# Decoder layer: the gated recurrence's x turned in 32x32 squares by VectorE, its norm factors spread by small products

## The chip, the cores and the metric

The kernel runs on one core of a Trainium2 chip. The metric is the device time of one execution in microseconds (us), lower is better. The core has TensorE (PE, with its weight loads PEld), VectorE (DVE), ScalarE (ACT), GpSimd (POOL) and SyncE (SP), which issues most of the DMAs.

## The reference, cut to what matters

A decoder layer on x of 2 x 2048 x 512 in float32: a gated recurrence, cross-attention, and a mixture of experts. The change touches the first part and the hand-over to the second:

```python
def _layernorm(x, axis=-1, eps=1e-05):
    m = jnp.mean(x, axis=axis, keepdims=True)
    v = jnp.var(x, axis=axis, keepdims=True)
    return (x - m) / jnp.sqrt(v + eps)
...
z = jax.nn.sigmoid(jnp.einsum('bsd,ndk->bsnk', x, Wz) + bz)   # x is layernorm(x) here
h_tilde = jnp.einsum('bsd,ndk->bsnk', x, Wh) + bh
a = (1.0 - z).reshape(b_, s_, d_)
bb = (z * h_tilde).reshape(b_, s_, d_)
_, h = jax.lax.associative_scan(_binop, (a, bb), axis=1)      # h_t = a_t h_(t-1) + bb_t
gate = jax.nn.sigmoid(jnp.einsum('bsd,de->bse', h, Wg) + bg)
return gate * h
```

## The kernel before, in words

The 4096 tokens are worked in 8 chunks of 512 (`NCH = 8`, c = 0 to 7), each of 4 tiles of 128 tokens (`TPC`, index j); the 512 features are 4 blocks of 128 (`KC`, index k for inputs and m for outputs). Every float32 product is done as three products of rounded parts (`TERMS`: high by high, high by low, low by high), so that one block m of z, of h or of the gate is 12 matmuls of 512 columns. ScalarE makes the high part (`hi_part`, L1218), VectorE the low part (`lo_part`, L1615).

The recurrence stage runs from the start to about 327 us. Its order is written out by hand, one list for each engine, tied by semaphores. For each chunk:

- TensorE does `z_and_h(c)`: z0, h0, two turned tiles of the gated rows of the chunk before (`gated_back`, L842), z1, h1, two more of them, z2, h2, z3, h3 (L716). Then `gates(c)`: two groups of transposes of the next chunk's normalised rows (`transpose_x`, L754), the gate products of blocks 0 and 1 without their last input block (18 matmuls, L781), their last input block (6 matmuls), which wait for the low part of h3, the other two groups of transposes, and blocks 2 and 3 (24 matmuls, L781). Block 2 goes into the bank of block 0 and so waits until ScalarE has read block 0 (`gate_ready`). `z_and_h(c + 1)` waits for the last low part of x.
- ScalarE, for each m: high part of h(m - 1), then the sigmoid of z(m) (L1284). Then high part of h3, high parts 0 and 1 of the next x, gate sigmoids 0 and 1 (L1301), high parts 2 and 3 of x, gate sigmoids 2 and 3, with pieces of the expert weights (`split_piece_hi`) between.
- VectorE, for each m: low part of h(m - 1), then `recurrence(c, m)`: b (L1680), a = 1 - z (L1683), the scan (L1686), the carry (L1689). Between them lie the residual rows and statistics of the chunk before. Then low part of h3, a weight piece, low parts 0 and 1 of x, `gated` 0 and 1 (L1714), low parts 2 and 3 of x, the rest, the statistics of chunk c + 2 (`ln1_stats`, L1646 to L1652) and its normalised rows (`ln1_apply`, L1658).
- GpSimd makes the inverse deviation (`ln1_pow`, L2564). SyncE moves weight pieces, rows of x and results; it also places the keys (`kblk`) at the start.

Chunk 0 has its own start: TensorE turns its x between the products of keys and values. The statistics of chunk 1 are taken in chunk 0, behind recurrence 1.

## Time and profile before

| | |
|---|---|
| median of 3 runs | 1172.0 us (1169.74 to 1174.47) |
| the profiled execution, its own time | 1170.26 us |
| its span, first to last instruction | 1168.5 us |
| mean granted TensorE clock | 0.991 |
| busy share of the span | PE 95%, DVE 78%, PEld 77%, ACT 62%, POOL 34% |
| one chunk of the recurrence | 36.57 us |

The span is 1.8 us short of the execution's own time. The shares are means over stages with different limits; for this change the recurrence stage alone is to be read.

### The profile page before, as it was taken

What the parts mean: (1) busy time and instruction counts of PE and PEld (TensorE: products, weight loads), DVE (VectorE), ACT (ScalarE), POOL (GpSimd) and SP (SyncE); (2) the same over time, 40 slices, a digit from 0 to 9 for tenths busy, and PEclk for the clock granted to TensorE, in tenths of its full rate; (3) what the DMA queues carried; (4) which work ended last, traced back from release to release, by engine and by line L of the source; (5) the groups of instructions that cost most, each with busy time, mean ns of one, the idle gap of its engine ahead of it and who ended that gap; (6) DMA issues with size and microseconds to landing.
All of it is one profiled execution on the core that took longest, in us unless ns stands there. A gap on an engine that the chain in (4) does not pass through costs nothing.

```text
span 1168.5 us, 24237 instructions
## 1 busy us (share of the span) xinstructions
PE 1108.3 (95%) x6017; PEld 905.0 (77%) x6018; DVE 910.5 (78%) x2172; ACT 722.2 (62%) x2148; POOL 393.4 (34%) x328
## 2 busy tenths in 40 slices
PE   6999999999989999999999888999999999999993
PEld 5888888888877787777777666777888888888882
DVE  6888888887874778878878877877777777777774
ACT  5223332233377777768676644866787787877873
POOL 3000000000034433545536364445534434443432
PEclk9999999999999999999999998999999999999998
DMA  8544545445340133143143377786555454444543
GB/s 261 163 149 159 190 148 173 151 163 207 126 147 1 57 89 111 56 124 100 46 145 90 128 206 219 201 249 152 94 85 81 81 85 80 86 81 81 88 63 40
DMA packets 95316, 144.76 MB, mean 124 GB/s; under 512 B 20864, under 2 KB 37428, under 8 KB 94607
## 3 DMA queue, kind: packets, MB, share of 16 engines
q1 hardware_dynamic: 77338, 106.83, 28.8%
q0 software_dynamic: 17216, 35.73, 17.4%
q10 hardware_dynamic: 693, 1.36, 0.4%
q8 instruction: 33, 0.54, 0.2%
q14 instruction: 36, 0.29, 0.1%
HBM read 82.69 MB, written 64.76 MB: 126 GB/s over the span
## 4 chain that ended last, share of the span: by engine, by line
PE 72%; DVE 9%; issue 7%; DMA 6%; ACT 3%; POOL 2%; DVEq 0%; POOLq 0%; ACTq 0%; SPq 0%
PE banks L1126 27%; PE banks L716 17%; PE banks L928 7%; PE banks L781 6%; DMA out<-rows,scatter_rows 4%; PE banks L893 3%; PE banks L906 3%; PE banks L1154 2%; PE banks L1138 2%; ACT rows L1335 2%; DVE operands L1615 2%; PE banks L917 1%; PE banks L754 1%; DVE rows L1917 1%; ACT operands L1218 1%
## 5 line engine op out<-in xcount | busy, mean ns | idle before, releaser
L1126 PE MATMUL banks<-operands 128*128 x1608 | 390.5, 398 | 9.2 <-ACT operands L1218 5.0
L1126 PEld LDWEIGHTS banks<-operands 128*128 128x128 f32 x1608 | 299.5, 190 | 73.9 <-issue 14.2
L716 PE MATMUL banks<-operands 128*128 128x512 f32 (+2 forms) x1224 | 290.1, 393 | 3.6 <-DVE operands L1615 3.6
L716 PEld LDWEIGHTS banks<-operands 128*128 128x128 f32 (+1 forms) x1224 | 226.1, 192 | 48.3 <-DVE operands L1615 3.7
L1218 ACT ACTIVATE operands<-banks 128x512 fp32r<-128x512 f32 (+1 forms) x232 | 137.6, 602 | 63.4 <-PE banks L807 34.2
L1615 DVE TENSOR_TENSOR operands<-banks,operands 128x512 fp32r<-128x512 f32 (+1 forms) x232 | 156.7, 683 | 15.6 <-ACT operands L1218 12.2
L1335 ACT ACTIVATE rows<-banks,score_shift 128x77 f32<-128x77 f32 x512 | 158.4, 337 | 11.2 <-DVE score_shift L1839 10.9
L2686 POOL DMA_INDIRECT out<-rows,scatter_rows x67 | 106.4, 1588 | 155.3 <-DVE rows L2419 109.7
L1218 ACT ACTIVATE operands<-rows 128x512 fp32r<-128x512 f32 (+2 forms) x77 | 54.0, 710 | 163.6 <-DVE rows L1686 139.4
L1540 ACT ACTIVATE banks<-banks,param_cols 128x128 f32<-128x128 f32 x268 | 99.2, 431 | 82.2 <-PE banks L1154 75.6
L2357 DVE BATCH_NORM_STATS2 moe_stats<-banks 128x6 f32<-128x512 f32 x134 | 93.2, 696 | 37.5 <-PE banks L1126 31.5
L2595 POOL TENSOR_TENSOR rows<-rows,score_rec 128x1232 f32<-128x1232 f32 x32 | 72.9, 2278 | 142.6 <-DVE score_rec L1847 142.6
L1335 ACT ACTIVATION_READ_ACCUMULATOR rows<-banks,score_shift 128x1 f32 x512 | 111.7, 218 | 0.0
L2660 POOL DMA_INDIRECT rows<-xf_rows,gather_rows x67 | 67.3, 1005 | 101.7 <-DVE gather_rows L2384 87.0
L928 PE MATMUL banks<-operands 128*128 128x512 f32 x384 | 94.2, 397 | 0.0
L781 PE MATMUL banks<-operands 128*128 128x512 f32 x384 | 91.9, 395 | 0.1
L781 PEld LDWEIGHTS banks<-operands 128*128 128x128 f32 x384 | 70.9, 188 | 15.8 <-DVE operands L1615 1.2
L928 PEld LDWEIGHTS banks<-operands 128*128 128x128 f32 x384 | 70.3, 188 | 14.9 <-DVE rows L1872 0.7
L906 PE MATMUL banks<-ident,rows 128*77 128x128 f32 x512 | 69.6, 276 | 11.3 <-DVE operands L1615 7.5
L906 PEld LDWEIGHTS banks<-ident,rows 128*77 128x77 f32 x512 | 58.4, 147 | 28.1 <-issue 13.7
L2569 POOL TENSOR_TENSOR ln_rstd<-ln_var_eps,minus_half 128x4 f32 (+1 forms) x8 | 10.1, 1260 | 181.1 <-DVE ln_var_eps L1710 181.1
L2608 POOL DMA_INDIRECT slot_table<-slot_payload,slot_rows x64 | 63.5, 991 | 19.2 <-issue 16.9
(191 smaller groups left out, 1603.1 us busy)
## 6 DMA issues: line engine op xcount, KB each, us to landing
expert_parts<-operands SPq DMA_DIRECT2D x32, 512.0 KB, 3.0
operands<-expert_parts SPq DMA_DIRECT2D x8, 2048.0 KB, 11.4
rows<-in_x SPq DMA_DIRECT2D x8, 1024.0 KB, 5.5
rows<-in_L_ffn_W SPq DMA_DIRECT2D x32, 256.0 KB, 3.6
x_rows<-rows SPq DMA_DIRECT2D x8, 1024.0 KB, 4.3
rows<-x_rows SPq DMA_DIRECT2D x8, 1024.0 KB, 6.2
xf_rows<-rows SPq DMA_DIRECT2D x32, 256.0 KB
out<-rows SPq DMA_DIRECT2D x32, 256.0 KB
```

What stands on the lines that cost most here:

```text
L716: last = nc.tensor.matmul(dst, stationary(a, k), moving(b, k), start=(t == 0 and k == 0), stop=(t == len(terms) - 1 and k == n_k - 1))
L781: last = nc.tensor.matmul(g_bank[m % 2], wg[:, a, k, m * P:(m + 1) * P], hTr[:, a2, k, :], start=(k == 0 and t == 0), stop=(k == KC - 1 an ...
L906: last = nc.tensor.transpose(tb(c, f"p{m}{hl}")[0:SK, j * P:(j + 1) * P], pb[m % 2][:, j, hl * SK:(hl + 1) * SK], ident[:, :])
L928: last = nc.tensor.matmul(mb(at, f"o{j}"), out_part(c, a, m)[:, j * P:(j + 1) * P], wo[:, a2, m, :], start=(m == 0 and t == 0), stop=(m == ...
L1126: last = nc.tensor.matmul(dst, stationary[:, a, k, :], weights[:, w, bass.ds(e, 1), a2, k, :].rearrange("p e f -> p (e f)"), start=False, ...
L1218: return nc.scalar.activation(dst, src, ACT.Copy, scale=scale)
L1335: nc.scalar.activation(pb[m % 2][:, j, keys], s_banks[:, j, keys], ACT.Exp, bias=nmax[:, m % 2, at], scale=-1.0, accum_out=ssum[:, m % 2, ...
L1540: nc.scalar.activation(ch_bank[:, at], ch_bank[:, at], ACT.Relu, scale=pcol[:, bass.ds(e * KC + (ROW_G1 + k), 1)], bias=pcol[:, bass.ds(e ...
L1615: return V.tensor_tensor(dst, src, hi.bitcast(F32), ALU.subtract)
L2357: V.bn_stats(c_st[:, which, :], src).then_inc(stat, 1)
L2595: G.tensor_tensor(p3, p3, srec[:, m % 2, :].unsqueeze(2).to_broadcast([P, TPC * HPG, SK]), ALU.mult).then_inc(p_ready, 1)
L2686: G.indirect_dma_start(out, bass.IndirectOffsetOnAxis(six[u][:, 0:1], 0), y2[u], None, compute_op=ALU.add).then_inc(added[u], 16)
```

## The change

- Rows of x are loaded a second time, in 32x32 squares (`load_squares`, four DMAs for each chunk into `xn`), from chunk 1 on. ScalarE normalises them in place (`normalise_x`): 4 x 4 activations of 128x128 with a scale and a bias, tiles 0 and 1 behind the sigmoid of z2, tiles 2 and 3 behind that of z3 (chunk 0: behind z3 and behind the high part of h3). VectorE turns them (`turn_x`): tiles 0 and 1 behind recurrence 3, tiles 2 and 3 behind the low part of h3 (chunk 0: all four there). `transpose_x` and `ln1_apply` are gone; chunk 0's own x is still turned by TensorE.
- The scale and bias of every row have to reach the partition of its square: GpSimd multiplies rstd with the negated mean, TensorE spreads both with four products of 8 columns (`spread_scales(c + 1)`, behind h1; in chunk 0 behind h2), VectorE copies the result out.
- a = 1 - z is made by ScalarE behind each sigmoid, into a tile of its own (`za_left`).
- The features of x come in another order, so Wz and Wh are loaded by 16 DMAs each in place of 4.
- The buffers of the squares lie where the keys are placed (`kblk`); the keys wait in DRAM (`kT_d`) and are placed in chunk 7, and GpSimd clears `kblk` there in two memsets.
- Some semaphores are merged (`passed`, `setup_t_done`, `ln1_stat`); their waits keep their places.

```diff
+
+
+        Q = nc.alloc_sbuf_tensor_at("recurrence_rows", [P, 77 * KB_ // 4], F32, offset=r_base + 48 * 1024)
+        xT_rows = Q[:, 0:KC * CH].rearrange("p (k t) -> p k t", k=KC)
+        sc1 = Q[:, 8 * KB_:8 * KB_ + 2 * TPC].rearrange("p (s j) -> p s j", s=2)
+        sc1_cols = Q[:, 8 * KB_:8 * KB_ + 2 * TPC]
+        sc_sq_cols = Q[:, 9 * KB_:9 * KB_ + 2 * CH // SQ]
+        sc_sq = sc_sq_cols.rearrange("p (b s j) -> p b s j", b=P // SQ, s=2)
+
+        spread = Q[:, 10 * KB_:12 * KB_].rearrange("p (b q r) -> p b q r", b=P // SQ, q=KC)
+        za_left = Q[:, 61 * KB_ // 4:77 * KB_ // 4].rearrange("p (i t) -> p i t", i=2)
...
             for raw, name, loaded in ((raw_wz, "L0_attn_Wz", wz_in), (raw_wh, "L0_attn_Wh", wh_in)):
                 for n in range(KC):
-                    sp.dma_start(raw[:, :, n * P:(n + 1) * P],
-                                 io[name][n].rearrange("(k p) f -> p k f", p=P)).then_inc(loaded, 16)
+                    for q in range(KC):
+                        sp.dma_start(raw[q * SQ:(q + 1) * SQ, :, n * P:(n + 1) * P],
+                                     io[name][n][q * P:(q + 1) * P, :].rearrange("(k r) f -> r k f", r=SQ)).then_inc(
+                            loaded, 16)
...
+            def load_squares(c):
+                src = x_sq[c] if isinstance(c, int) else x_sq[bass.ds(c, 1)].rearrange("c r b f -> (c r) b f")
+                for q in range(KC):
+                    sp.dma_start(xn[q * SQ:(q + 1) * SQ].rearrange("p j (b f) -> p (j b) f", f=P),
+                                 src[:, :, q * P:(q + 1) * P]).then_inc(xp_in, 16)
...
+                        sp.dma_start(kblk[rows, a, :, :, hl * SK:(hl + 1) * SK].bitcast(F32),
+                                     kT_d[rows, a]).then_inc(k_placed, 16)
...
             sp.wait_ge(k_lo, KC)
-            for hl in range(HPG):
-                rows = slice(hl * DH, (hl + 1) * DH)
-                for a in (HI, LO):
-                    sp.dma_start(kblk[rows, a, :, :, hl * SK:(hl + 1) * SK].bitcast(F32),
-                                 kT[rows, a].bitcast(F32)).then_inc(k_placed, 16)
+            sp.dma_start(kT_d, kT[:, :, :, :, :].bitcast(F32)).then_inc(k_placed, 16)
...
+            sp.wait_ge(a_t_done, KC)
+            load_squares(1)
...
             def a_chunk(c, first):
+                c_squares = not isinstance(c, int) or c < NCH - 2
...
+                    if n == 3 and c_squares:
+                        need_alone(sp, x_turned, 4 * (c + 1), passed)
+                        load_squares(c + 2)
+                    if n == 3 and isinstance(c, int) and c == NCH - 1:
+                        place_keys()
...
-            def transpose_x(c, ks=range(KC)):
-
+            def transpose_first(ks):
...
+            def spread_scales(c):
+
+                pe.wait_ge(ln1_rstd, rstd_steps(c))
+                need(pe, gate_ready, 4 * (c - 1))
+                for b in range(P // SQ):
+                    last = nc.tensor.matmul(g_bank[0][:, b * 2 * TPC:(b + 1) * 2 * TPC],
+                                            spread[:, b].rearrange("p q r -> p (q r)"), sc1_cols, start=True, stop=True)
+                last.then_inc(sc_done, 1)
+
             def z_and_h(c, back=True):
...
-                pe.wait_ge(a_t_read, t_group(c) + 4)
+                if isinstance(c, int) and c == 0:
+                    pe.wait_ge(a_t_read, KC)
+                else:
+                    pe.wait_ge(xnT_lo, 4 * c)
...
+                    if m == (1 if back else 2) and not (isinstance(c, int) and c == NCH - 1):
+                        spread_scales(c + 1)
...
-                if ahead:
-                    transpose_x(c + 1, (0, 1))
-                else:
+                if not ahead:
...
                     if m == 0:
+                        if ahead:
+                            pe.wait_ge(sc_in, c + 1)
...
                 pe.wait_ge(hT_lo, 4 * c + KC)
                 for m in range(2):
                     gate_terms(c, m, (KC - 1,)).then_inc(g_done, 1)
-                if ahead:
-                    transpose_x(c + 1, (2, 3))
-                else:
+                if not ahead:
                     x1_to_features(0, -1, (2, 3))
                 for m in range(2, KC):
                     pe.wait_ge(gate_ready, 4 * c + m - 1)
...
-            def x_hi(c, ks=range(KC)):
...
+            def x_hi(c, ks):
+                if ks[0] == 0:
+                    act.wait_ge(h_done, 4 * c)
+                    act.wait_ge(x_turned, 4 * c)
+                for k in ks:
+                    hi_part(xnT[:, HI, k, :], xT_rows[:, k, :]).then_inc(xnT_hi, 1)
+
+            def normalise_x(c, js):
+                for j in js:
+                    if j == 0:
+                        act.wait_ge(xp_in, 16 * KC * c)
+                        act.wait_ge(sc_in, c)
+                    for b in range(P // SQ):
+                        square = xn[:, j, b * P:(b + 1) * P]
+                        last = nc.scalar.activation(square, square, ACT.Identity, scale=sc_sq[:, b, 0, j:j + 1],
+                                                    bias=sc_sq[:, b, 1, j:j + 1])
+                    last.then_inc(xn_ready, 1)
...
                     need(act, h_ready, n - 1)
                     nc.scalar.activation(za[:, m % 2, :], z_bank[m % 2], ACT.Sigmoid,
                                          bias=pcol[:, ROW_BZ + m:ROW_BZ + m + 1]).then_inc(z_ready, 1)
+                    act.wait_ge(z_ready, n + 1)
+                    nc.scalar.activation(za_left[:, m % 2, :], za[:, m % 2, :], ACT.Identity, scale=-1.0,
+                                         bias=ones[:, 0:1]).then_inc(a_ready, 1)
+                    if not last:
+                        normalise_x(c + 1, ((), (), (), (0, 1))[m] if first else ((), (), (0, 1), (2, 3))[m])
...
                 h_hi(c, KC - 1)
+                if first:
+                    normalise_x(c + 1, (2, 3))
...
             def ln1_stats(c):
-                need(dve, xn_ready, 4 * c)
-                need_alone(dve, x_in, 16 * (c + 1), dve_passed)
+                need_alone(dve, x_in, 16 * (c + 1), passed)
                 for j in range(TPC):
...
-                need_alone(dve, ln1_stat, 4 * (c + 1), dve_passed)
+                need_alone(dve, ln1_stat, 8 * c + 4, passed)
+                need_alone(dve, xn_ready, 4 * c, passed)
+                if not (isinstance(c, int) and c < 2):
+                    need_alone(dve, sc_in, c - 1, passed)
                 for j in range(TPC):
-                    V.bn_aggr(mv1[:, j, :], st1[:, j, :]).then_inc(ln1_aggr, 1)
...
+                if not (isinstance(c, int) and c == 0):
+                    V.tensor_scalar(sc1[:, 1, :], mv1[:, :, 0], -1.0, None, ALU.mult)
                 V.tensor_scalar_add(ve1[:, :], mv1[:, :, 1], EPS).then_inc(ln1_eps, 1)
 
-            def ln1_apply(c):
-                dve.wait_ge(ln1_rstd, c + 1)
-                need(dve, a_t_done, t_group(c - 1) + 4 if not (isinstance(c, int) and c == 0) else 0)
+            def first_rows():
...
-                    V.tensor_scalar(xn[:, j, :], xr(c, j), mv1[:, j, 0:1], rs1[:, j:j + 1],
-                                    ALU.subtract, ALU.mult).then_inc(xn_ready, 1)
...
+            def turn_x(c, js):
+                for j in js:
+                    dve.wait_ge(xn_ready, 4 * c + j + 1)
+                    V.transpose(xT_rows[:, :, j * P:(j + 1) * P].rearrange("p k (b r) -> p b k r", r=SQ),
+                                xn[:, j].rearrange("p (b k r) -> p b k r", b=KC, k=KC)).then_inc(x_turned, 1)
...
+            def x_lo(c, ks):
                 for k in ks:
                     dve.wait_ge(xnT_hi, 4 * c + k + 1)
-                    lo_part(xnT[:, LO, k, :], t_bank[k % 2], xnT[:, HI, k, :]).then_inc(a_t_read, 1)
+                    lo_part(xnT[:, LO, k, :], xT_rows[:, k, :], xnT[:, HI, k, :]).then_inc(xnT_lo, 1)
...
@@ -1680,10 +1757,9 @@
                 V.scalar_tensor_tensor(zb, h_bank[m % 2], pcol[:, ROW_BH + m:ROW_BH + m + 1],
                                        za[:, m % 2, :], ALU.add, ALU.mult).then_inc(b_ready, 1)
                 dve.wait_ge(b_ready, n + 1)
-                V.tensor_scalar(za[:, m % 2, :], za[:, m % 2, :], -1.0, 1.0, ALU.mult, ALU.add).then_inc(a_ready, 1)
                 dve.wait_ge(a_ready, n + 1)
                 need(dve, carry_ready, n - 3)
-                V.tensor_tensor_scan(hT[:, m, :], za[:, m % 2, :], zb, carry_at(c, m, 0),
+                V.tensor_tensor_scan(hT[:, m, :], za_left[:, m % 2, :], zb, carry_at(c, m, 0),
                                      ALU.mult, ALU.add).then_inc(h_ready, 1)
...
                     if first and m == 1:
-                        dve.wait_ge(k_placed, 16 * 2 * HPG)
+                        dve.wait_ge(k_placed, 16)
+                        V.tensor_copy(spread, ident[:, :].rearrange("p (b r) -> p b r", r=SQ).unsqueeze(2).to_broadcast(
+                            [P, P // SQ, KC, SQ]))
                     if m:
                         h_lo(c, m - 1)
                     recurrence(c, m)
                     if first and m == 1:
                         ln1_stats(1)
+                    if ahead and m == (2 if first else 1):
+                        dve.wait_ge(sc_done, c + 1)
+                        V.tensor_copy(sc_sq_cols, g_bank[0][:, 0:CH // SQ * 2]).then_inc(sc_in, 1)
                     if m == (2 if first else 1):
                         split_piece_lo(c, 0)
-                    if first and m == 2:
-                        ln1_apply(1)
...
+                    if ahead:
+                        turn_x(c + 1, ((), (), (), ())[m] if first else ((), (), (), (0, 1))[m])
                 h_lo(c, KC - 1)
+                if ahead:
+                    turn_x(c + 1, (0, 1, 2, 3) if first else (2, 3))
                 split_piece_lo(c, 1)
...
-                if ahead >= 2:
-                    ln1_apply(c + 2)
...
             def ln1_pow(c):
                 pool.wait_ge(ln1_eps, c + 1)
-                need(pool, xn_ready, 4 * c)
-                G.tensor_tensor(rs1[:, :], ve1[:, :], half[:, 0:TPC], ALU.pow).then_inc(ln1_rstd, 1)
+                if isinstance(c, int) and c == 0:
+                    G.tensor_tensor(rs1[:, :], ve1[:, :], half[:, 0:TPC], ALU.pow).then_inc(ln1_rstd, 1)
+                    return
+                G.tensor_tensor(sc1[:, 0, :], ve1[:, :], half[:, 0:TPC], ALU.pow).then_inc(ln1_rstd, 1)
+                pool.wait_ge(ln1_rstd, rstd_steps(c) - 1)
+                G.tensor_tensor(sc1[:, 1, :], sc1[:, 1, :], sc1[:, 0, :], ALU.mult).then_inc(ln1_rstd, 1)
...
+            pool.wait_ge(xnT_lo, 4 * (NCH - 1))
+            G.memset(r_at(48, int(15.25 * KB_)).bitcast(F32), 0.0)
+            pool.wait_ge(h_ready, KC * NCH)
+            G.memset(r_at(63.25, 4 * KB_).bitcast(F32), 0.0).then_inc(pool_step, 1)
```

## Rows read from the trace of the kernel before

**Rows 1.** The page's first part, one engine: busy us, share, instructions.

```profile
PE 1108.3 (95%) x6017; PEld 905.0 (77%) x6018; DVE 910.5 (78%) x2172; ACT 722.2 (62%) x2148; POOL 393.4 (34%) x328
```

**Rows 2.** Busy time from behind h3 of chunk 1 to chunk 2's; clock, DMA share last.

```profile
88.05:124.62 36.57, 36.57 (x177) 30.37 (x176) 31.52 (x60) 12.26 (x22) 2.50 (x2) 1.00 0.48 165
```

**Rows 3.** Timeline of TensorE, chunk 2: start, us, work, count, idle before.

```profile
113.61 11.17 PE L716 MATMUL banks<-operands 128*128 128x512 f32 x48
124.62 1.03 PE L754 MATMUL banks<-ident,rows 128*128 128x128 f32 x8
125.62 5.78 PE L781 MATMUL banks<-operands 128*128 128x512 f32 x24
131.24 1.04 PE L754 MATMUL banks<-ident,rows 128*128 128x128 f32 x8
132.03 5.73 PE L781 MATMUL banks<-operands 128*128 128x512 f32 x24
```

**Rows 4.** Timeline of VectorE, the same chunk, behind h3.

```profile
125.48 0.75 DVE L1680 SCALAR_TENSOR_TENSOR rows<-banks,param_cols,rows 128x512 f32<-128x512 f32 x1
126.26 0.45 DVE L1683 TENSOR_SCALAR rows<-rows 128x512 f32<-128x512 f32 x1
126.85 1.28 DVE L1686 TENSOR_TENSOR_SCAN rows<-rows,carry 128x512 f32<-128x512 f32 x1
128.28 0.15 DVE L1689 COPY carry<-rows 128x1 f32 x1
128.84 1.29 DVE L1615 TENSOR_TENSOR operands<-rows,operands 128x512 fp32r<-128x512 f32 x2 [0.40 <-ACT operands L1218]
```

**Rows 5.** Timeline of ScalarE, the same chunk.

```profile
124.45 0.67 ACT L1284 ACTIVATE rows<-banks,param_cols 128x512 f32<-128x512 f32 x1
128.71 1.07 ACT L1218 ACTIVATE operands<-banks 128x512 fp32r<-128x512 f32 x2
130.75 1.38 ACT L1301 ACTIVATE rows<-banks,param_cols 128x512 f32<-128x512 f32 x2 [0.97 <-PE banks L781]
```

**Rows 6.** Groups by line behind 327 us: count, busy, mean ns, idle.

```profile
L1917 DVE STREAM_TRANSPOSE rows<-rows 128x512 f32<-128x512 f32 x24 | 15.4, 681 | 0.0
L1540 ACT ACTIVATE banks<-banks,param_cols 128x128 f32<-128x128 f32 x268 | 99.2, 431 | 82.2 <-PE banks L1154 75.6 <-issue 6.6
```

**Rows 7.** Timeline of TensorE: two narrow float32 products of a later stage.

```profile
433.58 0.29 PE L961 MATMUL banks<-gate_sel,before 128*128 128x16 f32 x2
...
433.95 1.09 PE L893 MATMUL banks<-operands 128*128 128x308 f32 x6
```

**Rows 8.** Timeline of TensorE, the start and chunk 0.

```profile
26.27 24.83 PE L716 MATMUL banks<-operands 128*77 128x512 f32 x108
50.94 1.77 PE L754 MATMUL banks<-ident,rows 128*128 128x128 f32 x8
...
58.90 1.40 PE L781 MATMUL banks<-operands 128*128 128x512 f32 x5
```

**Rows 9.** Timeline of VectorE in chunk 0.

```profile
34.88 0.75 DVE L1680 SCALAR_TENSOR_TENSOR rows<-banks,param_cols,rows 128x512 f32<-128x512 f32 x1 [1.57 <-PE banks L716]
...
46.07 0.17 DVE L1652 TENSOR_SCALAR ln_var_eps<-ln_mean_var 128x4 f32<-128x4 f32 x1
```

**Rows 10.** Timeline of GpSimd in chunk 0.

```profile
46.32 1.67 POOL L2564 TENSOR_TENSOR ln_rstd<-ln_var_eps,minus_half 128x4 f32<-128x4 f32 x1 [20.50 <-DVE ln_var_eps L1652]
```

**Rows 11.** Timeline of TensorE in the expert stage: 12 matmuls behind a wait.

```profile
708.00 4.50 PE L1126 MATMUL banks<-operands 128*128 x12 [2.22 <-ACT banks L1516]
...
737.08 3.00 PE L1126 MATMUL banks<-operands 128*128 x12 [0.89 <-ACT operands L1218]
```

**Rows 12.** Timeline of TensorE in chunk 7.

```profile
307.34 2.04 PE L807 MATMUL banks<-ident,rows 128*128 128x128 f32 x8
```

**Rows 13.** Timeline of SyncE's queue at the start.

```profile
12.30 4.97 SPq L464 DMA_DIRECT2D rows<-in_L_attn_Wh  x4
```

**Rows 14.** Timeline of ScalarE at the start.

```profile
18.38 1.92 ACT L1218 ACTIVATE operands<-rows 128x2048 fp32r<-128x2048 f32 x1 [2.15 <-DMA rows<-in_L_attn_Wz]
```

122 lines of the change are left out of this document (67 added, 55 removed).

## The prediction

> **What bounds the kernel now.** The page's first part comes first: TensorE is busy 95% of the span, VectorE 78% [rows 1]. That is a mean over stages, so the stretches come next. From behind h3 of chunk 1 to behind h3 of chunk 2, TensorE is busy 36.57 of 36.57 us, VectorE 31.52, ScalarE 12.26, at full clock [rows 2]. So TensorE sets the time of the recurrence stage, and a microsecond saved or lost in its row is one of the kernel's. VectorE, 86% busy, is near enough that where its work stands in its list decides. The timelines then show who is last at each turn [rows 3, 4, 5]. All times below are of chunk 2; T is the end of h3 in TensorE's row, 124.62.
>
> TensorE before: transposes of x from T to T + 1.00, gate blocks 0 and 1 to T + 6.62, transposes to T + 7.41, blocks 2 and 3 from there [rows 3]. One 512-column matmul advances the row by 11.01 / 48 = 0.23 us. ScalarE sigmoids gate 0 at 130.75, before TensorE wants its bank at 132.03 [rows 3, 5]. VectorE has the low part of h3 at about 129.5, TensorE wants it at about 125.62 + 18 x 0.23 = 129.8 [rows 3, 4]. So the transposes that go are work, but they also stand where TensorE would otherwise wait for the other two.
>
> **The steady chunk (1 to 6), part by part.** *Removed from TensorE:* 16 transposes, 1.00 + 0.79 = 1.8 us [rows 3].
>
> *Added to TensorE:* four float32 products of 8 columns. Two such products of 16 columns advance the row by 433.95 - 433.58 = 0.37 us [rows 7], so four cost 0.75; I take 0.8. Bounds 0.5 and 1.0: the columns are half as many, but the weights are as wide.
>
> *VectorE:* loses four times 0.43 (a = 1 - z, [rows 4]) and the four normalised rows, gains four turns of 15.4 / 24 = 0.64 [rows 6] and two small copies. It comes out a little lighter, and no longer runs behind the recurrences: in chunk 2 it began the last one at 125.48, 0.86 after T [rows 4]. The products of chunk 0 show how early it can begin: 36 matmuls from 26.27 end at 34.5, and b starts at 34.88, 0.35 later [rows 8, 9].
>
> *ScalarE:* gains 16 squares. The nearest row is the 128x128 activation with scale and bias, 99.2 / 268 = 0.37 us in a row of them [rows 6]; bounds 0.3 and 0.5. With four activations of 512 columns (0.6 each) this is 8.3 us in a chunk, on 12.3 busy of 36.57 [rows 2]. Behind z3 (T - 2.75, read from T - 2.4) stand the sigmoid 0.6, a 0.7, eight squares 3.0 and a weight piece 0.6: ScalarE is free at T + 2.5, when the scan of h3 ends. No loss; at 0.5 for a square it is T + 3.5, still hidden by VectorE's turning.
>
> The Trainium skill speaks against this move: its page ScalarE: Activation LUTs, section Rules for kernel authors, sends multiplies and adds to VectorE, and budgets 0.3 us for an activation plus 0.83 ns for an element, 0.41 us for a square. The trace agrees with its budget within a tenth (0.37 to 0.43), and by it the squares would cost 6.5 us of ScalarE in place of 5.9, with no change in the sum.
>
> *The new wait.* Follow VectorE and ScalarE from T, with the durations and gaps of [rows 4, 5, 6]:
> - b from T + 0.35 to 1.1; scan 1.25 to 2.55; carry to 2.85.
> - turns of tiles 0 and 1, 2 x 0.62: to 4.1. The high part of h3 is ready at 3.1, so it waits for the turns, not they for it.
> - low part of h3: to 4.8. TensorE has done its 18 matmuls at T + 4.15: it waits about 0.7, and its blocks 0 and 1 end at T + 6.2.
> - turns of tiles 2 and 3: to T + 6.05. Only now may ScalarE take the high parts 0 and 1 of x (they need all four tiles), 1.1 us: to 7.15; gate sigmoid 0: to 7.85.
> - TensorE's block 2 needs the bank that this sigmoid empties: it starts at T + 7.9 and waits 1.7.
>
> Before it started at T + 7.41. The 1.8 us that went out come back as waits of 2.4, so blocks 2 and 3 begin 0.5 later than before, and the spreading products come on top: a chunk takes 36.57 + 0.5 + 0.8 = 37.9, +1.3. Six chunks: **+7.8**. What stands behind is in time: low parts 2 and 3 of x at about T + 10.5, wanted at T + 13.5.
>
> *DMAs:* SyncE passes `x_turned` together with the weight piece behind it, which VectorE makes only after the turns, and issues four loads of squares. At the 1.24 us of each of the four Wh loads [rows 13] that is at most 5 us of queue, about T + 6.5 to T + 11.5. The squares are first read 30 us later. The expert piece queued behind them is read at about T + 14: hidden. The DMA engines are busy 0.48 [rows 2]; 1 MB more a chunk lifts that by a few tenths.
>
> **Chunk 0.** T here is 50.94 [rows 8]. The spreading products stand behind h2, at 26.27 + 84 x 0.23 = 45.5, but the statistics of chunk 1 are ready only at 46.07 + 0.17 [rows 9]. VectorE saves one 0.43 and gains a small product: 45.9. GpSimd's power takes 1.67 [rows 10]: 47.65. Its new product of 4 columns has no row; it lies between nothing and 1.67, I take 0.8 (same shape, simpler operation). TensorE spreads at 48.5, 3.0 us late, so T becomes 54.9: **+4.0**. Then all four tiles are turned behind h3: ScalarE's squares 0 and 1 wait for the scales and z3, squares 2 and 3 stand behind the high part of h3 and end at about 61.0; the last turn 61.7, high parts 62.8, sigmoid 63.5. Block 2 starts at T + 8.65 where it was 58.90 - 50.94 = 7.96 [rows 8]: **+0.7**, in a wait of 3.1.
>
> *The clock.* Behind a wait of 2.22 us, 12 matmuls take 4.50 us; behind one of 0.89 they take 3.00 [rows 11]. The longer wait cost 1.5 more behind it. Chunk 0 has two waits of 3.0, longer still: **+3.0**. A steady chunk's 0.7 and 1.7, apart by 1.4 of work, lie between the two rows; I take no fall, bounds 0 and 1.5.
>
> **The start.** Wz and Wh now come by 32 DMAs. The bytes and pieces are the same; four issues of Wh took 4.97 us [rows 13], and sixteen of a quarter's size take somewhat more. ScalarE already waited 2.15 for Wz [rows 14], and the low parts that start z0 follow closely. I take **+1.0**; bounds 0 and 3.
>
> **Chunk 7.** In its 2.04 us for 8 transposes of x1 against 1.03 in others [rows 3, 12] TensorE waits for VectorE's rows, and VectorE is lighter by 0.43 a block: **-1.0**, bounds -1.0 and 0. The keys are placed in this chunk, some 5.4 us of queue from about T + 7; TensorE wants them at about T + 17: nothing, but 2 or 3 us of cover.
>
> **The sum.** 7.8 + 4.7 + 3.0 + 1.0 - 1.0 = 15.5 on 1170.26 gives 1185.8. The median of the runs is 1.7 above that execution: 1187. What lies behind the recurrence stage is unchanged and starts later by the same.
>
> **The rivals.**
> 1. *The clock falls in every chunk* (0.18). The waits of 0.7 and 1.7 bring it down. For: the 4.50 behind 2.22. Against: the 3.00 behind 0.89 [rows 11]. Price 6 x 1.5 = 9: 1196. The Trainium skill, TensorE: Matmul & The Clock Gate, section The HAM clock gate, has the array fall to 1.2 GHz when it idles; the 4.50 us against 3.00 agree with the rule.
> 2. *The wait for gate 0 does not arise* (0.17). It would take ScalarE's sigmoid before T + 5.6, 2.3 us earlier than the list above gives. Then a steady chunk is 0.8 - 1.8 = -1.0, six -6; chunk 0 +4.0 - 2.4 + 1.5 of one fallen clock = 3.1; start +1, chunk 7 -1: -3, **1169**, no change.
> 3. *The same, and faster* (0.10): the sign turns when in addition the unknown prices lie at their low ends: GpSimd's product 0.1 in place of 0.8, nothing at the start, no fallen clock. That is -3.0 - 0.7 - 1.0 - 1.5 = -6.2: **1166**. Each steady chunk must then wait less than 0.1 in all. For it speaks that TensorE has 1.0 less to do in 36.57 us and VectorE is lighter; against it the order: two turns stand before the low part of h3 and four before the gate's sigmoid.
>
> **How the numbers follow.** The forecast (waits as worked out, clock falling in chunk 0 alone) has 0.55, with 1179 to 1192 as its own range: the steady chunk at +0.6 to +1.8 (squares 0.3 to 0.5, products 0.5 to 1.0), start 0 to 3. Two in ten lie outside 1170 to 1197. Half a per cent, 5.9 us, is about what a measurement of this kernel tells from no change. Faster 0.10; same (rival 2 and the low edge of the forecast) 0.18; slower 0.72.
>
> **What the changed profile would show.** TensorE idle twice in each `gates`: some 0.7 us before the last input block of blocks 0 and 1, released by the low part of h3, and 1.7 before block 2, released by the gate's sigmoid. The second is the heart: without it the forecast falls to rival 2. In chunk 0 an idle of 3 us before the spreading products, released by GpSimd. A granted clock below 1.00 in the steady stretches would say rival 1. A turn of far less than 0.64 us, or squares over 0.5, would move the waits by four or eight times the difference.

## The result, and the profile after

The changed kernel takes 1193.4 us (median of 4 runs, 1187.6 to 1197.3) against 1172.2 before: the ratio is 1.0183, 95% interval 1.0157 to 1.0210. The forecast was 1187, slower: 6 too low. The measured time lies 1.4 above the 1179 to 1192 that the prediction gave its main line, and inside its wider 1170 to 1197. The profiled execution took 1192.81 us, its span 1191.0, so 22.5 us more than the span before.

The page's first part after the change, to be held against [rows 1]:

```profile
PE 1110.4 (93%) x5961; PEld 904.5 (76%) x5962; DVE 906.1 (76%) x2155; ACT 788.9 (66%) x2292; POOL 397.0 (33%) x336
```

All shares fell by a little while the span grew: TensorE was given waits. The windows of the changed kernel say where. Columns: length; busy time of TensorE, its weight load, VectorE, ScalarE, GpSimd; granted clock; DMA share; GB/s. The second runs from h3 of chunk 1 to h3 of chunk 2 and answers to [rows 2]; the others are 4 us behind a wait in chunk 0 and in chunk 7.

```profile
53.00:57.00 4.00, 4.00 (x13) 3.47 (x14) 1.39 (x3) 0.23 (x1) 0.00 (x0) 0.50 0.19 70
102.01:140.00 37.99, 35.87 (x169) 29.43 (x168) 30.78 (x58) 21.46 (x42) 3.10 (x3) 1.00 0.61 186
331.00:335.00 4.00, 4.00 (x14) 3.35 (x15) 3.42 (x6) 1.50 (x3) 0.95 (x1) 0.57 0.07 28
```

This first steady chunk is 37.99 us long instead of 36.57 (the ones behind it 37.6 to 37.8) and TensorE is busy for 0.7 less in it, at a granted clock of 1.00 (the level of 2.4 GHz). In the other two TensorE is never idle, but at 0.50 (1.2 GHz) and 0.57.

TensorE's timeline of the changed kernel: first the start and chunk 0, then chunk 2 (T = 140.00), then chunk 7. In brackets stands the idle time before a group and what ended it.

```profile
31.25 18.00 PE L743 MATMUL banks<-operands 128*128 128x512 f32 x72 [2.55 <-DVE operands L1677]
52.61 1.88 PE L788 MATMUL banks<-recurrence_rows 128*128 128x8 f32 x8 [3.36 <-POOL recurrence_rows L2648]
54.34 7.49 PE L743 MATMUL banks<-operands 128*128 128x512 f32 x24
...
70.42 7.35 PE L820 MATMUL banks<-operands 128*128 128x512 f32 x24 [3.15 <-ACT rows L1363]
...
127.37 0.95 PE L788 MATMUL banks<-recurrence_rows 128*128 128x8 f32 x8
140.00 4.24 PE L820 MATMUL banks<-operands 128*128 128x512 f32 x18
144.75 1.66 PE L820 MATMUL banks<-operands 128*128 128x512 f32 x6 [0.50 <-DVE operands L1677]
147.78 5.75 PE L820 MATMUL banks<-operands 128*128 128x512 f32 x24 [1.37 <-ACT rows L1363]
...
327.32 0.38 PE L846 MATMUL banks<-ident,rows 128*128 128x128 f32 x2
330.49 1.54 PE L846 MATMUL banks<-ident,rows 128*128 128x128 f32 x6 [2.79 <-DVE rows L1803]
331.68 7.08 PE L820 MATMUL banks<-operands 128*128 128x512 f32 x24
```

Read chunk 2 first, against [rows 3]. The two groups of transposes of x are gone. In place of the first stands nothing, of the second two idle times: 0.50 before the last six matmuls of blocks 0 and 1 (VectorE's low part of h3), and 1.37 before block 2 (ScalarE's gate sigmoid). Block 2 starts at T + 7.78. Chunk 0 shows the same in larger: 3.36 for GpSimd's factors, 3.15 for the sigmoid, and behind each a group of 24 matmuls takes 7.3 to 7.5 us where it takes 5.6 at full clock.

Why the sigmoid is late is seen in the other engines' timelines. VectorE of the changed kernel behind h3 (compare [rows 4]):

```profile
140.26 0.75 DVE L1757 SCALAR_TENSOR_TENSOR rows<-banks,param_cols,rows 128x512 f32<-128x512 f32 x1 [1.57 <-PE banks L743]
141.15 1.28 DVE L1762 TENSOR_TENSOR_SCAN rows<-recurrence_rows,carry,rows 128x512 f32<-128x512 f32 x1
142.81 1.30 DVE L1730 STREAM_TRANSPOSE recurrence_rows<-rows 128x512 f32<-128x512 f32 x2
144.04 0.65 DVE L1677 TENSOR_TENSOR operands<-rows,operands 128x512 fp32r<-128x512 f32 x1
144.61 1.29 DVE L1730 STREAM_TRANSPOSE recurrence_rows<-rows 128x512 f32<-128x512 f32 x2
```

ScalarE of the changed kernel, the same place (compare [rows 5]):

```profile
138.90 3.18 ACT L1286 ACTIVATE rows<-rows,recurrence_rows 128x128 f32<-128x128 f32 x8
141.99 1.14 ACT L1255 ACTIVATE operands<-rows 128x512 fp32r<-128x512 f32 x2
146.00 1.15 ACT L1255 ACTIVATE operands<-recurrence_rows 128x512 fp32r<-128x512 f32 x2 [2.87 <-DVE recurrence_rows L1730]
147.06 1.25 ACT L1363 ACTIVATE rows<-banks,param_cols 128x512 f32<-128x512 f32 x2
```

The last turn ends at 145.90, T + 5.90, where the prediction had T + 6.05; ScalarE has stood still for 2.87 us and takes the high parts of x at 146.00; only then the two sigmoids, from 147.06; and TensorE goes on at 147.78. The sigmoid's bank was full before that: where it stands first in the list (experiment 1) it starts 1.00 behind the restart of TensorE's last six matmuls, which would be 145.75 here, 1.3 earlier. So an operand of the *next* chunk stands in ScalarE's list ahead of the gate that *this* chunk's next matmuls wait for.

**Where 23.7 us went**, read as differences of the starts of the same groups in TensorE's row, after minus before, up to the last gate block of chunk 7 (339.39 against 315.67):

| stretch | measured | forecast |
|---|---|---|
| start: z0 at 31.25 in place of 26.27 + 12 x 0.23 = 29.0; then 72 matmuls in 18.00 in place of 16.5 | +2.2, +1.5 | +1.0 |
| chunk 0: wait 3.4, spreading products 1.7, z3 and h3 at the low clock +1.8, gate products 15.94 in place of 13.5, +2.4 | +9.3 | +7.7 |
| chunks 1 to 6 (six recurrence steps) | +6.8 | +7.8 |
| chunk 7's gate products | +3.7 | -1.0 |

The stages behind it gave back 1.2, and 22.5 are left.

### The profile page after: what moved, and what is told of

Read it like the earlier page. It is cut to its first block, busy times and chain, and to the rows that moved or that the text cites. A ratio compares the mean times of both kernels' runs of the same rounds, so it can differ in the third digit from the quotient of the medians.

```text
span 1191.0 us, 24340 instructions
## 1 busy us (share of the span) xinstructions
PE 1110.4 (93%) x5961; PEld 904.5 (76%) x5962; DVE 906.1 (76%) x2155; ACT 788.9 (66%) x2292; POOL 397.0 (33%) x336
## 4 chain that ended last, share of the span: by engine, by line
PE 65%; DVE 10%; issue 8%; DMA 6%; ACT 4%; SPq 3%; POOL 2%; another core or an unknown queue 0%; DVEq 0%; POOLq 0%; ACTq 0%
PE banks L1163 25%; PE banks L743 18%; PE banks L965 5%; PE banks L820 4%; PE banks L930 3%; PE banks L943 3%; DMA rows<-slot_table 2%; DMA out<-rows,scatter_rows 2%; PE banks L1175 2%; PE banks L1191 2%; ACT rows L1397 2%; PE banks L954 1%; SPq L473 1%; ACT operands L1255 1%; DVE operands L1677 1%
## 5 line engine op out<-in xcount | busy, mean ns | idle before, releaser
L743 PE MATMUL banks<-operands 128*128 128x512 f32 (+2 forms) x1224 | 293.3, 396 | 6.1 <-DVE operands L1677 6.1
L1255 ACT ACTIVATE operands<-banks 128x512 fp32r<-128x512 f32 (+1 forms) x204 | 122.7, 605 | 65.7 <-PE banks L846 27.7
L1677 DVE TENSOR_TENSOR operands<-banks,operands 128x512 fp32r<-128x512 f32 (+1 forms) x204 | 138.6, 682 | 17.5 <-ACT operands L1255 15.6
L820 PE MATMUL banks<-operands 128*128 128x512 f32 x384 | 95.6, 403 | 14.0 <-ACT rows L1363 11.4
L965 PE MATMUL banks<-operands 128*128 128x512 f32 x384 | 93.7, 396 | 0.0
L930 PE MATMUL banks<-operands 128*128 128x308 f32 x384 | 70.1, 316 | 0.0
```

Of the source, the lines that this page charges most:

```text
L743: last = nc.tensor.matmul(dst, stationary(a, k), moving(b, k), start=(t == 0 and k == 0), stop=(t == len(terms) - 1 and k == n_k - 1))
L820: last = nc.tensor.matmul(g_bank[m % 2], wg[:, a, k, m * P:(m + 1) * P], hTr[:, a2, k, :], start=(k == 0 and t == 0), stop=(k == KC - 1 an ...
L930: last = nc.tensor.matmul(s_banks[:, j, :], qT[:, a, m, j * P:(j + 1) * P], keys, start=(t == 0), stop=(t == len(TERMS) - 1 and not masked ...
L965: last = nc.tensor.matmul(mb(at, f"o{j}"), out_part(c, a, m)[:, j * P:(j + 1) * P], wo[:, a2, m, :], start=(m == 0 and t == 0), stop=(m == ...
L1255: return nc.scalar.activation(dst, src, ACT.Copy, scale=scale)
L1677: return V.tensor_tensor(dst, src, hi.bitcast(F32), ALU.subtract)
```

## The experiments

All are edits of the changed kernel, except the one that says otherwise. Times are medians, with the kernel before measured beside them: 1174.1 us for the first four, 1172.5 for the next four, 1171.6 for the last three. "Last block" is where the 24 gate products of blocks 0 and 1 of chunk 7 start: 309.31 before, 331.68 after. It leaves out the later stages. It is read from one execution of each kernel, and so holds that execution's start too: z0 began between 30.4 and 33.7 in edits that don't touch what stands before it, and 72 matmuls behind it took 16.6 in some and 18.0 to 18.2 in others.

**1. gate_first: the sigmoid ahead of the high parts.** My theory: the steady loss is the order in ScalarE's list, and not the work.

```diff
-                    elif m % 2 == 0:
+                    elif m == 2:
...
+                    if m == 0 and not last:
+                        x_hi(c + 1, (0, 1))
```

> The changed kernel with one reordering: ScalarE takes the sigmoid of gate 0 before the high parts 0 and 1 of the next x. Theory (TensorE's block 2 waits for that sigmoid, and the sigmoid for the last turn): the wait of 1.37 us in every steady chunk and of 3.15 us in chunk 0 goes, with the slow matmuls behind the latter (24 in 7.35 us in place of 5.7). That is 6 x 1.37 + 3.15 + 1.65 = 13.0 us, so about 1180. Rival (VectorE's list is the limit, whichever wait shows it): the wait moves to z0, which needs all low parts of x, and the time stays within 3 us of 1193.

Measured: 1183.4 us, ratio 1.0075 (1.0046 to 1.0104), last block at 319.83, 11.9 earlier. Of these, 1.4 are not the edit's: the 72 matmuls behind z0 took 16.60 in this execution, not 18.00. TensorE's timeline of this kernel, chunk 0 and chunk 2 (T = 134.35):

```profile
67.37 5.75 PE L820 MATMUL banks<-operands 128*128 128x512 f32 x24 [1.13 <-ACT rows L1363]
...
134.35 4.24 PE L820 MATMUL banks<-operands 128*128 128x512 f32 x18
139.10 7.47 PE L820 MATMUL banks<-operands 128*128 128x512 f32 x30 [0.51 <-DVE operands L1679]
```

The wait of 1.37 is gone as an idle time, that of 0.51 stays, and 30 matmuls run in one piece. They take 7.3 us up to z0 where 30 steps of 0.23 are 6.9: block 2's first product starts at 140.84, 0.47 behind the one before it, because the sigmoid (140.10, 0.69 long) ends only then. So about 0.35 of the wait is left inside the piece. A steady chunk is 1.2 us shorter, not 1.37. In chunk 0 the wait falls from 3.15 to 1.13, and the 24 matmuls behind it take 5.75 in place of 7.35, at full clock. The theory holds; the 13.0 that it forecast came as about 10.5 in the stage.

**2. clear_early: GpSimd's clearing 26 us earlier.** In chunk 7 TensorE waits 2.79 for VectorE's normalised rows. VectorE's and GpSimd's timelines of the *changed* kernel there, and what the view by source line says of that line (lowest, median, highest ns):

```profile
325.85 5.03 DVE L1803 TENSOR_SCALAR rows<-rows,ln_mean,ln_rstd 128x512 f32<-128x512 f32 x4
326.76 3.40 POOL L2668 MEMSET operands<- 128x3904 f32 x1
L1803 DVE TENSOR_SCALAR rows<-rows,ln_mean,ln_rstd x32: 452/536/3668, 325.9 to 638.5; 128x512 f32<-128x512 f32 x24, 128x512 f32 x8
```

One of 32 such instructions took 3668 ns. It starts at 326.76, as does a memset of 3.40 us that stands behind GpSimd's power, and ends 0.27 us behind it. Theory: the memset holds it up. Rival: VectorE is late for another reason.

```diff
-            ln2_pow(NCH - 2)
             pool.wait_ge(xnT_lo, 4 * (NCH - 1))
             G.memset(r_at(48, int(15.25 * KB_)).bitcast(F32), 0.0)
+            ln2_pow(NCH - 2)
```

> The changed kernel with GpSimd's large clearing of the key blocks (3.40 us) ahead of the inverse deviation of chunk 6, so that it no longer runs beside VectorE's normalised rows in chunk 7. Theory (VectorE and GpSimd hold each other up: one tensor_scalar of 512 columns took 3.67 us in place of 0.54): the four rows take 2 us in place of 5.03, TensorE's wait of 2.79 us in chunk 7 falls to about 0.3, and the 24 matmuls behind it take 5.8 in place of 7.08: -4 us, 1189. Rival (VectorE waited for a DMA or for the deviation, and the clearing only happened to run then): no change.

Measured: 1192.2 us, ratio 1.0148 (1.0103 to 1.0193), where 1189 was expected: the medians can't tell it from the changed kernel. The place itself is clear. TensorE, VectorE and GpSimd of clear_early:

```profile
326.80 1.26 PE L846 MATMUL banks<-ident,rows 128*128 128x128 f32 x8
327.99 5.72 PE L820 MATMUL banks<-operands 128*128 128x512 f32 x24
...
325.33 1.91 DVE L1803 TENSOR_SCALAR rows<-rows,ln_mean,ln_rstd 128x512 f32<-128x512 f32 x4
...
300.29 3.37 POOL L2667 MEMSET operands<- 128x3904 f32 x1 [10.87 <-DVE operands L1677]
301.42 0.69 DVE L1790 TENSOR_TENSOR rows<-rows 128x512 f32<-128x512 f32 x1 [1.19 <-ACT rows L1363]
302.02 0.69 DVE L1677 TENSOR_TENSOR operands<-rows,operands 128x512 fp32r<-128x512 f32 x1
```

The four take 1.91 in place of 5.03, TensorE doesn't wait, and the 24 matmuls take 5.72 in place of 7.08. The theory holds, and not by one execution: TensorE's wait at this place is 2.79 in four more edits that leave the memset where it was and 3.25 in a fifth, and it is gone in all five that move it. The memset is as long as it was (3.37), and the two operations of two inputs that now run beside it take their usual 0.69.

Chunk 0 of the same trace shows something else:

```profile
71.42 5.74 PE L820 MATMUL banks<-operands 128*128 128x512 f32 x24 [3.12 <-ACT rows L1363]
```

Nothing was changed there, and the wait before block 2 is as long as in the changed kernel (3.15). Yet the matmuls behind it ran at a granted clock of 1.00 (2.4 GHz), 5.74 in place of 7.35. So a wait of 3.1 us lowers the clock behind it in most executions (five of six here), not in each.

**3. stats_early: chunk 1's statistics and the spread copy behind the first recurrence**, not the second, so that GpSimd can begin earlier.

```diff
-                    if first and m == 1:
+                    if m:
+                        h_lo(c, m - 1)
+                    recurrence(c, m)
+                    if first and m == 0:
                         dve.wait_ge(k_placed, 16)
...
-                    if m:
-                        h_lo(c, m - 1)
-                    recurrence(c, m)
-                    if first and m == 1:
                         ln1_stats(1)
```

> The changed kernel with the statistics of chunk 1 behind the first recurrence of chunk 0 in place of the second (and the spread pattern with them). Theory (TensorE waits 3.36 us in chunk 0 for GpSimd's factors, which come 3.9 us behind the statistics, and its clock falls there): the wait goes, with the slow matmuls behind it (1.88 us for the spreading products in place of 0.95, 7.49 for 24 matmuls in place of 5.6): 3.4 + 0.9 + 1.9 = 6.2 us, 1187. Rival (the second load of x or the rows of chunk 1 come too late for it, since SyncE's queue is 5 us behind the kernel before): VectorE waits for them, delays recurrence 1, and less than 2 us is won.

Measured: 1190.9 us, ratio 1.0141 (1.0115 to 1.0168), last block at 326.83. Chunk 0 of stats_early:

```profile
33.74 16.59 PE L743 MATMUL banks<-operands 128*128 128x512 f32 x72 [1.78 <-DVE operands L1677]
50.18 0.95 PE L788 MATMUL banks<-recurrence_rows 128*128 128x8 f32 x8
50.98 5.75 PE L743 MATMUL banks<-operands 128*128 128x512 f32 x24
65.32 7.35 PE L820 MATMUL banks<-operands 128*128 128x512 f32 x24 [3.15 <-ACT rows L1363]
```

No wait for GpSimd; the products take 0.95 in place of 1.88 and the 24 matmuls 5.75 in place of 7.49. From z0 to T it is 56.57 - 33.74 = 22.8 us in place of 30.4. Of these 7.6, 1.4 belong to the 72 matmuls behind z0 (16.59 in place of 18.00), which the edit doesn't touch; 6.2 are left, as forecast. In this execution z0 came 2.5 us later, so the last block is only 4.9 earlier. The ratio fell by 0.0042, also 4.9 us, with intervals that overlap; 6.2 was expected.

**4. a_on_vector: a = 1 - z back to VectorE.** Theory: ScalarE has idle time at the place, VectorE's list is the chain, so moving work *to* VectorE lengthens the chunk although ScalarE gets free. Rival: ScalarE's load (the squares) is what makes the sigmoid late.

```diff
-                    nc.scalar.activation(za_left[:, m % 2, :], za[:, m % 2, :], ACT.Identity, scale=-1.0,
-                                         bias=ones[:, 0:1]).then_inc(a_ready, 1)
...
+                V.tensor_scalar(za_left[:, m % 2, :], za[:, m % 2, :], -1.0, 1.0, ALU.mult, ALU.add).then_inc(a_ready, 1)
```

> The changed kernel with a = 1 - z back on VectorE (0.43 us for each block) and no such activation on ScalarE (0.63 us each). Theory (VectorE's list from h3 to the last turn is the chain): both waits of each gate stage move 0.45 us later, so six steady chunks and chunk 0 cost 7 x 0.45 = 3 us more, 1196. Rival (ScalarE, with 16 squares and these activations, is the limit): ScalarE is 0.6 us earlier behind z3, and the time falls by 2 us or more.

Measured: 1203.5 us, ratio 1.0235 (1.0202 to 1.0268), where 1196 was expected; last block at 337.31. TensorE of a_on_vector, with T = 143.09:

```profile
148.16 1.66 PE L820 MATMUL banks<-operands 128*128 128x512 f32 x6 [0.83 <-DVE operands L1674]
151.20 5.75 PE L820 MATMUL banks<-operands 128*128 128x512 f32 x24 [1.37 <-ACT rows L1360]
```

Block 2 starts at T + 8.11 in place of 7.78: the first wait grew by 0.33 and the second is the same, with less work on ScalarE. Over the steady chunks it is 0.1 to 0.5 a chunk more, 0.34 in the mean. The rival is out. The size was missed: the recurrence stage accounts for 5.6 us more (1.4 of it a later z0 in this execution), and the later stages took another 5.5 that I can't place.

**5. squares_early: squares behind z1 and z2, two turns behind the third recurrence**, so that the turns are over when h3 comes.

```diff
-                        normalise_x(c + 1, ((), (), (), (0, 1))[m] if first else ((), (), (0, 1), (2, 3))[m])
+                        normalise_x(c + 1, ((), (), (), (0, 1))[m] if first else ((), (0, 1), (2, 3), ())[m])
...
-                        turn_x(c + 1, ((), (), (), ())[m] if first else ((), (), (), (0, 1))[m])
+                        turn_x(c + 1, ((), (), (), ())[m] if first else ((), (), (0, 1), (2, 3))[m])
                 h_lo(c, KC - 1)
-                if ahead:
-                    turn_x(c + 1, (0, 1, 2, 3) if first else (2, 3))
+                if ahead and first:
+                    turn_x(c + 1, (0, 1, 2, 3))
```

> The changed kernel with the squares one block earlier in every chunk but chunk 0: normalised behind z1 and z2, turned behind recurrences 2 and 3, all four ahead of the low part of h3. Theory (the gate's sigmoid waits for the last turn): the last turn ends at 4.1 us behind h3 in place of 6.0, the sigmoid of gate 0 is in time, and the wait of 1.37 us goes from six chunks: -8 us, 1185; the wait of 0.5 for the low part of h3 stays. Rival (ScalarE is now the limit: its squares behind z1 wait for the scales, and it comes late to z2): the wait appears before a product of h or z instead, and the time stays near 1193.

Measured: 1207.9 us, ratio 1.0286 (1.0249 to 1.0323), a miss by 23. TensorE, ScalarE and VectorE of squares_early:

```profile
144.04 13.21 PE L820 MATMUL banks<-operands 128*128 128x512 f32 x48 [3.19 <-DVE operands L1677]
...
171.88 3.19 ACT L1286 ACTIVATE rows<-rows,recurrence_rows 128x128 f32<-128x128 f32 x8 [4.09 <-DVE recurrence_rows L1834]
...
175.62 0.69 DVE L1677 TENSOR_TENSOR operands<-rows,operands 128x512 fp32r<-128x512 f32 x1 [3.84 <-ACT operands L1255]
```

All 48 gate products now run in one piece, so both old waits are gone; but 3.19 us stand before them, and the clock falls behind it (0.50 in the stretch from 146 to 148; 13.21 for 48, 11.2 at full clock). The chain is read back from the bottom: VectorE waits 3.84 for the high part of a weight piece; ScalarE makes that piece behind the squares; and the squares wait 4.09 for the scales, which VectorE copies only after recurrence 1. A chunk takes 40.8 us. The expectation's rival had named the wait for the scales, but with a time near 1193; that it holds up VectorE too, through the weight piece, neither had.

**6. before_16_loads: the kernel *before*, with each load of Wz and Wh cut into four of 32 partitions.** It measures that part of the start by itself.

```diff
-                    sp.dma_start(raw[:, :, n * P:(n + 1) * P],
-                                 io[name][n].rearrange("(k p) f -> p k f", p=P)).then_inc(loaded, 16)
+                    for q in range(KC):
+                        sp.dma_start(raw[q * SQ:(q + 1) * SQ, :, n * P:(n + 1) * P],
+                                     io[name][n].rearrange("(k p) f -> p k f", p=P)[q * SQ:(q + 1) * SQ]).then_inc(
+                            loaded, 16)
```

> The kernel before with one thing of the change: Wz and Wh by 16 DMAs each of 32 partitions in place of 4 of 128, same bytes, rows in the old order. Theory (the loads' issue made the start later): z0 begins 2 to 3 us later than at 29.0, and the time rises by 2 to 4 us to about 1177. Rival (the start is late for another part of the change, the permuted rows of chunk 0 or the keys' way over DRAM): no change that can be measured.

Measured: 1174.4 us, ratio 1.0018 (0.9997 to 1.0039). The time can't be told from no change, so this run decides nothing by its time; the traces are what is left to read. SyncE's queue of the changed kernel, which answers to [rows 13]:

```profile
4.93 10.13 SPq L473 DMA_DIRECT2D rows<-in_L_attn_Wz  x16
15.11 7.55 SPq L473 DMA_DIRECT2D rows<-in_L_attn_Wh  x16
```

and Wz's issues and z0 in before_16_loads:

```profile
4.93 9.01 SPq L465 DMA_DIRECT2D rows<-in_L_attn_Wz  x16
...
30.23 22.06 PE L718 MATMUL banks<-operands 128*128 128x512 f32 x96 [0.80 <-DVE operands L1617]
```

Sixteen issues of Wh take 7.55 us where four took 4.97, and z0 starts at 30.23, 1.2 later than before. That z0 hangs on them is seen in the chain of waits of the changed kernel, whose lines are start, us and what; the last load of Wh lands at 24.14, and z0 follows at 31.25 through ScalarE's and VectorE's parts of it:

```profile
22.22 1.92 DMA rows<-in_L_attn_Wh
...
26.47 1.23 DVE operands L1881 x4
...
29.82 1.29 DVE operands L1677 x2
31.25 4.86 PE banks L743 x14
```

The other traces bear this out. The queue's last issue of Wh ends at 21.53 in before_16_loads, at 22.66 in the changed kernel, and between 21.80 and 25.16 in seven of its edits (all of which have the same 32 loads); z0 starts 8.6 to 8.7 us behind that end in all nine. (In two more edits TensorE's own earlier work ends later still.) In the kernel before it ends at 17.27, and ScalarE takes Wh without a wait. So both parts of the start's 2.2 are this queue: with 32 loads it holds z0 back by 1.2 in before_16_loads, and the other 1.0 is that the same number of issues took 1.1 longer in the changed kernel's execution (Wz 10.13 against 9.01). Where SyncE alone issues them, Wz's 16 took between 9.0 and 11.1 from one trace to the next; why is not shown.

**7 and 8. best and best_pool.** The first joins experiments 1 to 3 with the early squares and only the first turn early; the second lets GpSimd issue Wh's 16 loads, to empty SyncE's queue. Both hold the early squares of experiment 5, whose result was not known yet.

> The changed kernel with all repairs: gate sigmoid 0 ahead of the high parts of x, the large clearing ahead of the deviation, the statistics of chunk 1 behind recurrence 0, squares normalised behind z1 and z2, tiles 0 and 1 turned behind recurrence 2 and tiles 2 and 3 behind the low part of h3. Theory: the prices add up (13.0 + 4 + 6.2, and 0.5 for the other wait in six chunks, 3): 1193.4 - 26 = 1167, with a steady chunk of 36.57 - 1.8 + 0.8 = 35.6 us. Rival (with both waits gone, ScalarE or VectorE is the next limit): a chunk of 36.5 us or more, 1172.

> The kernel with all repairs, and the 16 loads of Wh issued by GpSimd, which stands idle then, beside SyncE's 16 of Wz. Theory (the issue of 32 loads one after the other makes Wz and Wh late): z0 starts 1 to 3 us earlier and the time falls by as much, to 1165. Rival (at the start the DMA engines are full, so the order of landing decides and not the issue): Wh lands earlier, but x, Wv or Wz later, and nothing is won or the start is later.

Measured: best 1197.6 us, ratio 1.0220 (1.0180 to 1.0260), a miss by 30, with 3.20 us of wait before the 48 gate products, as in experiment 5. best_pool 1202.9, ratio 1.0257 (1.0221 to 1.0293), with the same wait. ScalarE and GpSimd's own queue of best_pool:

```profile
20.30 1.91 ACT L1255 ACTIVATE operands<-rows 128x2048 fp32r<-128x2048 f32 x1 [10.80 <-DMA rows<-in_L_xattn_bv]
...
3.15 8.95 POOL L2644 DMA_DIRECT2D rows<-in_L_attn_Wh  x16
```

Wh's issues ended at 12.1, but Wv came later: ScalarE waited 10.80 for it in place of 4.96 in best, and z0 slid to 35.12 from 30.49. The core's DMA engines were busy all the time from 3 to 12 us in both kernels (a share of 1.0 in each stretch of 3 us), so what is sent earlier puts something else off. That is the expectation's rival: the order of landing decided, and a second issuing engine didn't help.

**9. turn_in_gap: experiments 1 to 3, and two turns ahead of the last recurrence**, where VectorE waits 1.57 for h3 anyway, with the squares left where the change has them.

```diff
+                    if ahead and m == 3 and not first:
+                        turn_x(c + 1, (0, 1))
                     recurrence(c, m)
...
-                    if ahead:
-                        turn_x(c + 1, ((), (), (), ())[m] if first else ((), (), (), (0, 1))[m])
```

> The changed kernel with gate sigmoid 0 ahead of the high parts of x, the large clearing ahead of the deviation, the statistics of chunk 1 behind recurrence 0, the squares normalised where the change has them, and tiles 0 and 1 turned ahead of recurrence 3, where VectorE stands idle 1.57 us waiting for h3, in place of behind it. Theory: the wait of 0.5 for the low part of h3 goes too, VectorE's list behind h3 is 1.24 us shorter, and a steady chunk takes 36.57 - 1.8 + 0.8 = 35.6 us; 1183.4 of the run with the sigmoid moved, less 4 (clearing), 3 to 6 (statistics) and 3 to 5 (steady chunks) is 1169 to 1172. Rival: recurrence 3 now starts late, or the low parts of x are late for z0, and a chunk stays at 36.4 us.

**10. all_three: experiments 1 to 3 alone.**

> The same without the moved turns: tiles 0 and 1 behind recurrence 3 as in the change. Theory: the wait of 0.5 stays, a chunk takes 36.4 to 36.5 us, and the time is 3 to 5 us above the run with the turns in the gap. Rival: no difference between the two.

Measured: turn_in_gap 1171.7 us, ratio 0.9989 (0.9970 to 1.0007); all_three 1171.5, ratio 0.9993 (0.9971 to 1.0014). From h3 of chunk 2 to h3 of chunk 6 a chunk takes 36.0 to 36.2 us in turn_in_gap, 36.3 to 36.5 in all_three; the one before, from chunk 1 to 2, takes 36.9 in both. TensorE of turn_in_gap behind one h3 and in chunk 7:

```profile
127.53 4.24 PE L820 MATMUL banks<-operands 128*128 128x512 f32 x18
131.94 7.49 PE L820 MATMUL banks<-operands 128*128 128x512 f32 x30 [0.16 <-DVE operands L1679]
...
308.01 5.73 PE L820 MATMUL banks<-operands 128*128 128x512 f32 x24
```

The last block of chunk 7 starts at 308.01, 1.3 us before the kernel before and 23.7 before the change. Some 1.6 of the 23.7 lie in and just behind the start, which the edits leave alone (z0 0.2 earlier, its 72 matmuls in 16.57); the other 22 are undone by where four things stand. The 0.3 to 0.4 us a chunk that turn_in_gap wins over all_three can't be seen in the medians, so their time is that of experiment 10's rival (no difference). The 1169 to 1172 expected of turn_in_gap was met, though its steady chunk stayed above the 35.6 forecast. These are the two best kernels of the study, and neither can be told from the one before.

**11. spread_twice: each spreading product made twice.** Theory: they stand on the path and are paid in full. Rival: they fill time in which TensorE waits anyway.

```diff
-                for b in range(P // SQ):
+                for b in list(range(P // SQ)) * 2:
```

> The changed kernel with the four spreading products done twice, to the same place. Theory (they cost their 0.8 us in TensorE's row and everything behind h3 follows): 7 x 0.8 = 5.6 us more, 1199. Rival (TensorE waits 1.9 us for others in each chunk anyway, so its own extra work is hidden): less than 2 us.

Measured: 1200.2 us, ratio 1.0233 (1.0197 to 1.0269); by the ratios 5.9 above the changed kernel, where 5.6 was expected. TensorE of spread_twice:

```profile
130.25 1.84 PE L788 MATMUL banks<-recurrence_rows 128*128 128x8 f32 x16
```

Sixteen records take 1.84 where eight took 0.95, the waits behind h3 are as long as they were (0.50 and 1.37), and a chunk takes 38.5 to 38.9 in place of 37.6 to 38.0: the products are paid in full.

## Why the prediction was right, and where it was not

**The steady chunk: right, in mechanism and nearly in size.** The two idle times are there, released by the named instructions: 0.37 to 0.75 in place of 0.7 for the low part of h3, 1.37 in place of 1.7 for the sigmoid, block 2 at T + 7.8 in place of 7.9. Between T of chunk 1 and T of chunk 6 five chunks take 188.78 us after and 182.96 before: 5.8 more, 1.16 a chunk, where 1.3 was forecast. Experiment 1 shows the sigmoid's half and experiment 11 the products' share of 0.8. Squares take 3.18 / 8 = 0.40 us (0.37 assumed), spreading products 0.81 (0.8), turns 0.65 (0.64).

**That ScalarE had room for the squares: right.** Experiment 4 freed ScalarE and the sigmoid came no earlier. By the Trainium skill, ScalarE: Activation LUTs, section Rules for kernel authors, with its 0.3 us and 0.83 ns an element, a square is estimated at 0.41 us; that is nearer to the 0.40 measured than the 0.37 of the row that I took, and neither changes the sum.

**Chunk 0: right in kind, 1.6 too low.** The wait for GpSimd was 3.36 (3.0 forecast); its product of 4 columns took 1.00 (0.8). Block 2 came at T + 8.75 (8.65). I had not counted that the spreading products, too, run at the low clock: 1.73 in place of 0.81.

**The clock: right in chunk 0 in this execution, missed in two other places.** Rival 1 is out, the steady stretches have 1.00. That chunk 0 fell both times is not certain from one execution to the next: clear_early kept the full clock behind the second wait. But TensorE was also at the low level behind the 2.55 us before z0 (72 matmuls in 18.00 in place of 16.5) and behind the 2.79 of chunk 7 (+1.35). Experiments 1, 2 and 3 each shorten or remove one such wait, and the time behind it comes back each time; behind the waits of 1.13 to 1.18 before block 2 of chunk 0 (five edits) the clock stayed full, behind those of 3.1 to 3.3 it fell in five kernels of six.

**The start: mis-sized by 2.7,** 1.0 forecast, 2.2 and 1.5 of clock behind it measured, together 3.7, above the bound of 3 that I gave. I priced the issues on the queue, but not that a later z0 means a longer idle TensorE ahead of it. Experiment 6 shows 1.2 of it with the loads alone, and the ends of the queue in the other traces put the rest on the same queue. What makes that queue 1 to 3 us longer in one execution than in another stays open, and with it how much of the 2.2 and of the 1.5 another execution would show: only two of the ten edits of the changed kernel had a fallen clock behind z0.

**Chunk 7: the step that failed.** The prediction said: "TensorE waits for VectorE's rows, and VectorE is lighter by 0.43 a block: -1.0, bounds -1.0 and 0". It measured +3.7. I had the moved placing of the keys in view as DMA work only, not the clearing of their 3904 columns on GpSimd that now runs in this chunk beside VectorE's normalisation. Experiment 2 shows it: 3.2 us of hold-up and 1.35 of clock come back when the memset stands elsewhere. What the prediction did reason about was nearly right: without the memset the 8 transposes and their wait take 1.19 in place of 1.97, a gain of 0.8 where 1.0 was forecast.

**Rivals 2 and 3** (no wait for the sigmoid) are out for the change as it is. gate_first meets rival 2's condition, and took 1183.4, not 1169: a steady chunk came to 36.3 to 36.9 and not to the 35.6 that the rival had, and the start and chunk 7 cost what they did. That all_three (1171.5) came near 1169 is luck: it has two repairs more, which rival 2 knew nothing of. The change's own gain on TensorE (1.8 out, 0.8 in, 1.0 a chunk) is mostly spent: in the later steady chunks of all_three 0.5 goes into the wait for the low part of h3 and some 0.4 into the last of the sigmoid's, in turn_in_gap 0.2 and 0.4; the rest is eaten by the later start and by the spreading products and waits of chunk 0.

**In sum,** the forecast was 15.5 and 22.5 came. Of the difference of 7, chunk 7 makes 4.7, the start 2.7 and chunk 0 1.6; the steady chunks (-1.0) and the later stages (-1.2) go the other way.
